# Reordering the first routing of a macaron block and moving VectorE work to GpSimd and ScalarE

## The reference

```
x = x + 0.5 * L0_ffn(layernorm(x))    # 8 experts, 2 per row, d_ff 512
x = x + L0_attn(layernorm(x))         # 16 heads of 8, softmax over 256 keys
x = x + 0.5 * L0_ffn(layernorm(x))    # the same experts again
x = x + 0.5 * L1_ffn(layernorm(x))    # channel mix with the row before, r * (relu(k)^2 Wv)
x = x + L1_attn(layernorm(x))         # gated Toeplitz product by FFT along the sequence
x = x + 0.5 * L1_ffn(layernorm(x))
```

## Time and profile before

| | us |
|---|---|
| median of 3 runs | 720.45 (718.42 to 724.24) |
| the profiled execution | 716.23 |
| its span in the trace | 714.5 |
| PE, DVE, ACT, POOL busy | 603.1, 458.4, 336.7, 300.2 |

### The profile page before, as it was taken

The page is one execution under the profiler, slowest core; times in us unless marked ns, Lnnn a source line. Parts: engine busy times, 40 slices in busy tenths (PEclk is TensorE's granted clock), DMA queues, the critical chain, the costliest instruction groups (busy, mean ns, idle before and its releaser), DMA issues.

```text
span 714.5 us, 12146 instructions
## 1 busy us (share of the span) xinstructions
PE 603.1 (84%) x4067; PEld 472.4 (66%) x4067; DVE 458.4 (64%) x1226; ACT 336.7 (47%) x808; POOL 300.2 (42%) x396
## 2 busy tenths in 40 slices
PE   3516998897999898899988977999899899987795
PEld 3514787776897554555445644699688788966694
DVE  3896753342586765878887663368335587688675
ACT  2641443442464567546653243644243457445434
POOL 2634646566582502120010252254567574763251
PEclk9555899998999999879997585999899999998698
DMA  8611102111400000201000020014111300020000
GB/s 304 194 58 52 38 20 41 34 38 37 119 26 20 30 1 9 63 1 31 1 30 1 4 63 18 21 20 140 38 34 46 93 24 20 24 75 22 9 1 30
DMA packets 30459, 32.70 MB, mean 46 GB/s; under 512 B 5408, under 2 KB 24256, under 8 KB 30400
## 3 DMA queue, kind: packets, MB, share of 16 engines
q1 hardware_dynamic: 23648, 19.68, 8.5%
q0 software_dynamic: 5888, 12.07, 6.7%
q10 hardware_dynamic: 864, 0.18, 0.1%
HBM read 20.64 MB, written 11.27 MB: 45 GB/s over the span
## 4 chain that ended last, share of the span: by engine, by line
PE 63%; DVE 15%; another core or an unknown queue 5%; POOL 5%; issue 5%; ACT 4%; DMA 3%; SPq 1%; ACTq 0%; DVEq 0%
PE bank L1800 10%; PE bank L1709 9%; PE bank L1716 5%; PE bank L1859 5%; PE bank L1815 4%; PE bank L1850 3%; PE bank L1831 3%; PE bank L1782 3%; PE bank L1789 3%; PE bank L1763 3%; PE bank L1784 3%; PE bank L1787 2%; PE bank L1783 2%; PE bank L1788 2%
## 5 line engine op out<-in xcount | busy, mean ns | idle before, releaser
L1150 POOL DMA_INDIRECT XROW<-rows_in,of x92 | 91.6, 996 | 75.0 <-PE bank L1709 30.6
L1157 POOL DMA_INDIRECT rows_out<-OROW,to x92 | 93.1, 1012 | 68.6 <-DVE OROW L1559 46.6
L1547 DVE TENSOR_TENSOR SGA<-bank,SGA 128x512 f32<-128x512 f32 x92 | 62.4, 687 | 76.4 <-PE bank L1789 49.9
L1800 PE MATMUL bank<-WD,AT 128*128 x736 | 96.9, 279 | 0.9 <-DVE AT L1551 0.9
L1591 DVE TENSOR_REDUCE BIG<-bank 128x4 f32<-128x1024 f32 x64 | 77.4, 1222 | 29.7 <-PE bank L1831 29.5
L1800 PEld LDWEIGHTS bank<-WD,AT 128*128 128x128 f32 x736 | 92.2, 195 | 3.9 <-issue 1.3
L1246 ACT ACTIVATE SGA<-bank 128x512 f32<-128x512 f32 x92 | 54.7, 600 | 65.6 <-PE bank L1784 47.2
L1289 ACT ACTIVATE BIG<-bank 128x1024 f32<-128x1024 f32 x64 | 64.9, 1022 | 42.4 <-PE bank L1850 39.1
L1250 ACT ACTIVATE AT<-bank 128x512 f32<-128x512 f32 x58 | 34.5, 597 | 60.6 <-PE bank L1709 33.1
L1110 POOL TENSOR_SCALAR stats<-stats 128x4 f32<-128x4 f32 (+1 forms) x15 | 3.6, 238 | 135.4 <-DVE stats L1381 128.5
L1709 PE MATMUL bank<-ident,SGA 128*128 128x128 f32 x368 | 54.3, 277 | 3.2 <-DVE AT L1551 2.2
(11 more groups left out here) (224 smaller groups left out, 1359.3 us busy)
## 6 DMA issues: line engine op xcount, KB each, us to landing
rows_in<-HROW SPq DMA_DIRECT2D x16, 256.0 KB
GO<-rows_out SPq DMA_DIRECT2D x16, 256.0 KB
BIG<-in_w_e_dram SPq DMA_DIRECT2D x7, 512.0 KB, 10.1
WD<-in_w_e_dram SPq DMA_DIRECT2D x1, 2048.0 KB, 17.8
XROW<-rows_in,of POOLq DMA_INDIRECT x92
rows_out<-OROW,to POOLq DMA_INDIRECT x92
X<-in_x_dram SPq DMA_DIRECT2D x4, 256.0 KB, 8.6
out_dram<-X SPq DMA_DIRECT2D x8, 128.0 KB, 1.9
```

The costliest lines, as they stand in the source:

```text
L1150: gp.indirect_dma_start(cut(v.xrow[st.to.i], u % 4), None, v.hs[k], bass.IndirectOffsetOnAxis(ap=v.of[k % 2][:, u:u + 1], axis=0)).then_in ...
L1157: gp.indirect_dma_start(v.outs[k], bass.IndirectOffsetOnAxis(ap=v.to[k % 2][:, u:u + 1], axis=0), cut(v.orow[st.xt.i], u % 4), None).then_ ...
L1547: ve.tensor_tensor(a, bk[:, :], a, ALU.mult).then_inc(s["gated"], 1)
L1800: x = pe.matmul(cut(bk, u % 4), cut(v.aT[st.xt.i], f), cut(mine, f), start=(f == 0), stop=(f == 3))
```

## The change

- **Order.** `RANKS` becomes a list by group. Routing of group 0 and the constants have rank -29; the first quad has 3 - 30 = -27. `k_diag` to `k_enorm`, `decayed` and the `prep` of tiles 2 and 3 no longer start by the clock but when the first quad's `x_lo` is planned (mark "begun"). `prep(0)` and `prep(1)` start at 4.3 and 9.6. A pair of tiles counts as picked after `g_pick`, no longer after `g_mix`; the small gating tensors are doubled for this.
- **Choice of engine.** A wish may name a second operation (`other`). Whichever engine the plan finds free first takes it, ACT before DVE before POOL: `n_apply` or `n_pool` (POOL), `s_apply` or `s_pool` (POOL), `h_rows` or `h_act` (ACT).
- **p_lo moves.** ACT writes a second scaled copy of the projected bank (`p_raw`, 128x512), and POOL adds it to the rounded one. The ring of q and k pairs has three instead of four; the memory goes to two `raw` tiles.
- **Splits.** DVE and POOL make 8 remainders each (11 and 5 before). Rank 0 instead of 3.
- **r_place** handles both picks in one product and one sum: 13 operations instead of 15.
- **Tables.** `QUOTA` of exp 2 instead of 6, `PATIENCE` 0.3 instead of 1.0.

```diff
-QUOTA = {"silu": 2, "exp": 6}
-PATIENCE = 1.0
-RANKS = {"route": -6.0, "route1": 0.0, "combine": -3.0, "quads": 3.0, "settle": 2.0, "attention": -6.0, "experts": 0.0, "layer": 0.0}
+QUOTA = {"silu": 2, "exp": 2}
+PATIENCE = 0.3
+RANKS = {"split": 0.0, "decayed": 0.0, "route": [-29.0, 0.0, -6.0, -6.0], "quads": [3.0, 4.0, 9.0, 3.0],
+         "experts": [0.0, 0.0, 0.0, 1.0], "settle": [10.0, 9.0, 3.0, 0.0],
+         "combine": [-3.0, -3.0, -3.0, 12.0], "attention": [-6.0, -6.0], "layer": [0.0, -4.0]}
...
-        st = yield from self.add("n_apply", {"to": self.xns}, q=c, own=own, src=st)
+        st = yield from self.add("n_apply", {"to": self.xns}, "n_pool", q=c, own=own, src=st)
...
-        yield 40.0
+        self.begin(self.scales())
+
+    def scales(self):
+        yield from self.until("begun")
...
-            st = yield from self.add("w_lo2" if (2 * e + j) % 3 == 2 else "w_lo", e=e, j=j, src=st)
+            st = yield from self.add("w_lo2" if j else "w_lo", e=e, j=j, src=st)
...
+        elif k < 2:
+            yield 4.3 + 5.3 * k
         else:
-            yield 4.0 + 1.5 * k + 3.0 * (k > 1)
+            yield from self.until("begun")
...
-        st = yield from self.add("h_rows", bank=bk, to=h, own=own, src=st)
+        st = yield from self.add("h_rows", {}, "h_act", bank=bk, to=h, own=own, src=st)
...
+        if n == 0:
+            self.mark("begun", st)
...
+                raw = yield from self.add("p_raw", {"xt": self.raws}, j=j, bank=mm.bank, src=mm)
                 st = yield from self.add("p_hi", take, j=j, bank=mm.bank, src=mm, **to)
...
-                st = yield from self.add("p_lo", j=j, bank=mm.bank, src=st, **to)
-                self.banks.give(mm.bank, st)
+                st = yield from self.add("p_lo", j=j, xt=raw.xt, src=st, **to)
+                self.raws.give(raw.xt, st)
...
     def decayed(self):
 
-        yield 20.0
+        yield from self.until("begun")
...
-        st = yield from self.add("s_apply", {"to": self.xnq}, n=n, q=q, src=st)
+        st = yield from self.add("s_apply", {"to": self.xnq}, "s_pool", n=n, q=q, src=st)
...
+            for t in range(4):
+                x = gp.tensor_scalar(cut(v.xn[st.to.i], t), v.X[:, 4 * q + t, :], v.st2[i][:, t, 0:1],
+                                     v.rs[i][:, t:t + 1], ALU.subtract, ALU.mult)
...
+            gp.tensor_tensor(x[:, :], v.raw[st.xt.i][:, :], x[:, :].bitcast(F32), ALU.add).then_inc(s["p_lo"], 1)
...
+            for t in range(4):
+                x = act.activation(cut(v.hrow[st.to.i], t), cut(bk, t), ACT.Copy, scale=v.zr[st.own.i][:, t:t + 1])
...
-            for i in range(2):
-                chain(ve.tensor_tensor(v.r64, v.picks[k % 2][i], te, ALU.mult))
-                chain(ve.tensor_reduce(v.rplace[:, 8 * i:8 * i + 8], v.r64, AX.X, ALU.add))
+            chain(ve.tensor_tensor(v.r128, v.picked[k % 2], te.unsqueeze(1).broadcast_to([128, 2, 8, E]), ALU.mult))
+            chain(ve.tensor_reduce(v.rplace.rearrange("p (i t) -> p i t", i=2), v.r128, AX.X, ALU.add))
```

More of the change, by code:

```diff
@@ L56 @@
  d_turn .23 d_mm .45 c_mm .9 s_turn .23 m_mm 1.0 m_vmm .45 y_uv .9 y_dft 1.8 y_idft 1.8 y_turn .23 y_mm .45""",
-    "ACT": """k_evac .3 k_comb .3 k_enorm .6 n_evac .6 z_ss 1.9 w_hi .63 x_hi .7 silu .6 a_act .6 o_ss 1.9 g_tanh .25
- p_ss 1.9 p_T .7 p_hi .78 v_rows .6 st_exp 1.03 os_out .6 cc_evac .6 d_sig .3 d_ln .3 d_exp .6 d_act .3
+    "ACT": """k_evac .3 k_comb .3 k_enorm .6 n_evac .6 z_ss 1.9 h_act 1.2 w_hi .63 x_hi .7 silu .6 a_act .6 o_ss 1.9 g_tanh .25
+ p_ss 1.9 p_T .7 p_raw .7 p_hi .78 v_rows .6 st_exp 1.03 os_out .6 cc_evac .6 d_sig .3 d_ln .3 d_exp .6 d_act .3
  d_evac .4 d_silu .3 c_evac .4 s_evac .4 m_left .9 m_gate 1.2 y_silu .6 y_fw .6 y_evac .4""",
     "DVE": """k_scale .1 k_counts .4 k_diag 1.4 n_stats 1.4 n_apply 1.15 g_copy .3 h_rows 1.15 g_rank 2.1 g_pick 1.2 g_mix .3
- r_scan .3 r_place 5.2 r_hot .6 r_ids .8 r_tables 1.4 x_lo .75 w_lo .7 gated .7 a_dve .7 o_rows 1.6 mix 2.7 p_x 1.15 p_lo .75 mx_max 1.23 nm_add .41
+ r_scan .3 r_place 4.6 r_hot .6 r_ids .8 r_tables 1.4 x_lo .75 w_lo .7 gated .7 a_dve .7 o_rows 1.6 mix 2.7 p_x 1.15 mx_max 1.23 nm_add .41
  cc_part .6 at_x .7 d_gamma .2 d_in .2 d_stats .6 d_rows 1.2 d_tt .4 omega .1 s_stats 1 s_apply .7 m_mix .95 m_out .85
  y_prods 1.4 y_prod .95 y_gate .4 y_x .4""",
-    "POOL": """n_rstd 1.3 z_rstd 1.3 w_lo2 1.6 fetch 1.27 o_rstd 1.3 spread 1.27 p_rstd 1.3 d_rstd 1 s_rstd 1
+    "POOL": """n_rstd 1.3 n_pool 1.8 s_pool .95 p_lo 1.45 z_rstd 1.3 w_lo2 1.6 fetch 1.27 o_rstd 1.3 spread 1.27 p_rstd 1.3 d_rstd 1 s_rstd 1
  m_zero .1 y_cross 1.8""",
@@ L164 @@
     at: float = 0.0
+    other: str = None
 class Plan:
@@ L224, in go_on @@
             return
+        rank = self.rank
         if isinstance(until, float):
@@ L229, in go_on @@
             self.wishes[LENGTH[until.do][0]].append(until)
+            if until.other:
+                self.wishes[LENGTH[until.other][0]].append(until)
         else:
@@ L240, in serve @@
         one = min(ready, key=lambda w: (w.at + w.rank, w.number))
-        self.wishes[engine].remove(one)
+        self.wishes[LENGTH[one.do][0]].remove(one)
+        if one.other:
+            self.wishes[LENGTH[one.other][0]].remove(one)
+            if LENGTH[one.other][0] == engine:
+                one.do = one.other
         slots = {}
@@ L271, in slot, with add @@
         return min(free, key=lambda s: s.done)
-    def add(self, do, take={}, **what):
+    def add(self, do, take={}, other=None, **what):
+        self.number += 1
+        wish = Wish(do, 0, self.number, None, take, other=other)
+        slots = yield wish
+        do = wish.do
         engine, length = LENGTH[do]
-        self.number += 1
-        slots = yield Wish(do, 0, self.number, None, take)
         at = self.count[do] = self.count.get(do, 0) + 1
@@ L463, in quads @@
             g, i = divmod(n, QUADS)
+            if n:
+                self.rank = RANKS["quads"][g]
             ids = yield from self.until(("routed", g))
@@ L634, in projects @@
         for c in range(4):
+            self.rank = RANKS["attention"][c // 2]
             yield from self.project(c)
@@ L640, in attention @@
         for u in range(32):
+            self.rank = RANKS["attention"][u // 16]
             ev = yield from self.until(("projected", u // 2))
@@ L889, in layer @@
         for q in range(8):
-            self.begin(self.sequence(q))
+            self.begin(self.sequence(q), RANKS["layer"][q // 4])
 def the_plan():
     p = Plan()
-    p.begin(p.constants(), 0.0)
-    p.begin(p.decayed(), 0.0)
+    p.begin(p.constants(), RANKS["route"][0])
+    p.begin(p.decayed(), RANKS["decayed"])
     for e in range(E):
-        p.begin(p.split(e), 3.0)
+        p.begin(p.split(e), RANKS["split"])
     for g in range(4):
-        p.begin(p.route(g), RANKS["route1" if g == 1 else "route"])
-        p.begin(p.experts(g), RANKS["experts"])
-        p.begin(p.combine(g), RANKS["combine"])
-    p.begin(p.quads(), RANKS["quads"])
-    p.begin(p.attention(), RANKS["attention"])
-    p.begin(p.layer(), RANKS["layer"])
+        p.begin(p.route(g), RANKS["route"][g])
+        p.begin(p.experts(g), RANKS["experts"][g])
+        p.begin(p.combine(g), RANKS["combine"][g])
+    p.begin(p.quads(), RANKS["quads"][0] - 30.0)
+    p.begin(p.attention())
+    p.begin(p.layer(), RANKS["layer"][0])
     p.run()
@@ L1135, in gpsimd_program @@
             root(v.rs[i], v.var[i], v.st2[i][:, :, 1], 1.0, EPS_LN, 4).then_inc(s["n_rstd"], 1)
+        elif st.do == "n_pool":
+            i = st.own.i
+            w.wait_ge(s["n_rstd"], st.src.at)
+            w.wait_ge(s[st.to.by], st.to.at)
+            for t in range(4):
+                x = gp.tensor_scalar(cut(v.xn[st.to.i], t), v.X[:, 4 * q + t, :], v.st2[i][:, t, 0:1],
+                                     v.rs[i][:, t:t + 1], ALU.subtract, ALU.mult)
+            x.then_inc(s["n_pool"], 1)
+        elif st.do == "s_pool":
+            w.wait_ge(s["s_rstd"], st.src.at)
+            w.wait_ge(s[st.to.by], st.to.at)
+            for t in range(2):
+                x = gp.tensor_scalar(cut(v.xnq[st.to.i], t), v.X[:, 2 * q + t, :], v.q2[n][:, t, 0:1],
+                                     v.qrs[n][:, t:t + 1], ALU.subtract, ALU.mult)
+            x.then_inc(s["s_pool"], 1)
+        elif st.do == "p_lo":
+            w.wait_ge(s["p_hi"], st.src.at)
+            x = v.trips[st.to.i][st.j]
+            gp.tensor_tensor(x[:, :], v.raw[st.xt.i][:, :], x[:, :].bitcast(F32), ALU.add).then_inc(s["p_lo"], 1)
         elif st.do == "z_rstd":
```

96 lines of the change are left out of this document (53 added, 43 removed).

## The result

The changed kernel takes 726.13 us in the median of five runs (721.49 to 727.24), the kernel before 719.38 on the same chip (710.49 to 724.24, five runs). I had forecast 701. The profiled execution took 721.49, its span 719.7.

A forecast was written before the change was run, and what follows sets the result against it. Start bound by waits for VectorE, experts by TensorE, attention by neither fully; -19.8 + 8 + 3 - 6 - 4 = -18.8 from 716.2 gives 697.4, plus 4.2 for a median 701.6, given as 701; range 690 to 711.

The forecast's parts named there:

- Part 3, p_lo: Attention: low parts leave VectorE for GpSimd, ScalarE's extra passes hidden, longer pair latency covered; -4 us.
- Part 1, the start: Up to the first expert product: earlier root, gating, scan and routing bring it from 74.9 to 55.1, 19.8 us gained.
- What is paid back: Experts' stretch: held back work returns where TensorE is full, +8 us, and table loads between silus, +3.
- Part 2, quota: Start of attention: with exp quota 2, group 1's last block gets in some 19 us earlier, worth -6 us.
- Part 4: The end: `s_pool` and the last group's ranks move order only; 0, between -3 and +12 us.
- The slower one: Attention's projections: POOL, busy with group 2's fetches, delays chunk 3's `p_lo`; +32 us, 738; chance 0.10.
- The port: Attention's routings: GpSimd work on the port shared with VectorE stretches some 13 VectorE operations; +13 us, 714; chance 0.10.
- The last combine's late results: The end: the last combine's rank of 12 lets up to 12 us of other work go ahead; 713; chance 0.10.
- More: Attention: VectorE's relief and earlier tiles keep TensorE's clock up, gaining 15 us more; 686 or less; chance 0.14.

The follow-up runs named there:

- x3: Kernel before with only the low parts' move (`p_raw` on ScalarE, `p_lo` on GpSimd, three pairs), quiet chip: 695.10 us, ratio 1.034.
- x1: Kernel before, unchanged, on the quiet chip: 668.03 us, ratio 0.995.
- x2: Changed kernel, unchanged, on the quiet chip: 688.52 us, ratio 1.026.
- x4: Changed kernel with the low parts back on VectorE and four pairs, quiet chip: 673.20 us, ratio 1.000.
- The third round: Changed kernel without `s_pool`, 725.75 us; that with settling ranks of before, 735.21; kernel before with `s_pool`, 719.05; changed kernel unchanged, 723.99.
- e4: Kernel before with the new start alone, old quota and patience, low parts and norms on VectorE, quiet chip: 702.95 us, ratio 1.048.
- s1: Changed kernel without `s_pool`, so the layer's norms are all on VectorE: 725.75 us, ratio 1.009.
- e2: Changed kernel with the last group's and the layer's ranks of before, quiet chip: 689.36 us, ratio 1.033.
- s2: Kernel before with `s_pool` offered for `s_apply` and nothing else: 719.05 us, ratio 1.015.
- e1: Changed kernel without `n_pool` and `s_pool`, every norm on VectorE, quiet chip: 709.55 us, ratio 1.063.

## Why the prediction was wrong, step by step

- **Part 3, p_lo: the step that failed.** I took -4 from a range of -20.8 to 0, with the longer latency "covered, unless POOL is late". Measured +23 alone and +15 within the change (quiet chip): my range had no positive end, since I took the longer way of a pair and ScalarE's 32 passes as covered and hidden. I had read the maxima's 25.9 us of waits for TensorE as "the relief is worth little", and not drawn the other conclusion: in a stretch in which no engine is full, each waits for the others, and an edit that adds work and way between them can lose. In x3, 10 us of the loss are TensorE's idle time and 16 its lower clock (183.05 and 171.26 busy at 0.89 and 0.79 lose 20 and 36 us). How the edit makes TensorE idle stays open. The longer way alone is not shown to do it: from a pair's first projection to its second low part it is 1.7 us more in the mean (11.1 for 9.4, x3 and x1) and 1.3 (10.3 for 9.0, x2 and x4), not the 2.8 that I had estimated, because a low part on VectorE had begun only 0.8 to 1.0 us after its rounded tile (median of 32) and on GpSimd begins 0.1 us after it; and TensorE waited 0.8 us for low parts in x3. The waits that grew are for ScalarE's exponentials and VectorE's maxima, and in which of the three ways (ScalarE's passes, the pair's way, the new order) the edit lengthens them no run separates.
- **Part 1, the start.** First product -15.2 for -19.8. Root and gating came earlier than forecast (17.5, 18.9), but two tiles' gating took 13.5 us, not 8.4: four weight remainders of 0.6 stand between its steps, and three operations are stretched from 0.42 to 1.4 or 1.5, each beside a remainder of GpSimd (from 20.55 and from 26.49). `r_place` took 6.0 for 4.4, the inversions 8.3 for 8.1, and from there to the product 11.0 for 12.5. The trace thus agrees at the start with what the Trainium skill ("SBUF — State Buffer", "SBUF: two separate sides") says of the port pair that VectorE and GpSimd share, and more of it was on the path than the single row I had counted.
- **What is paid back.** 11 forecast, leaving 9; at block 23 8.6 us of the 15.2 were paid back and 6.6 left (7.6 and 7.2 on the quiet chip), so this term was too large rather than too small. On the quiet chip (x1, x2) TensorE is busy 33.05 and 19.80 us up to the first product, and from it to block 23:

```profile
74.65:142.96 68.31, 68.28 (x442) 60.79 (x442) 35.70 (x84) 31.94 (x80) 42.91 (x49) 0.96 0.16 38
59.82:135.80 75.98, 74.87 (x490) 65.90 (x490) 51.66 (x170) 42.97 (x115) 48.60 (x58) 1.00 0.19 45
```

  Some 13.3 us of work at the low clock were moved and 6.6 came back at the full one, half, as I had told; TensorE's idle time up to block 23 hardly changed (41.6 and 41.1). What the sum had wrong is that the 9 us would reach the end. Tile 0's first result already comes 2 to 3 us later than before (206.5 for 203.7; 189.5 for 187.3), and in x4, without the low parts' move, the layer is reached 1 us later than in x1. The third round shows that the settling rank holds tile 0 back, and also that taking it away gains nothing. The table loads fell between silus just as told, six of them, 7.7 us of ScalarE.
- **Part 2, quota.** Mechanism right (14 and 11 us earlier), value 1 us alone instead of 6: even the later result (323.4 without the edit) was there before attention's second chunk ended at 347.9, so nothing waited for it. Whether it matters when the start is moved is not shown: e4, which kept the old quota, got the block only at 296.
- **Part 4.** 0 forecast; the layer stretch takes 144 us in the changed kernel for 136 to 140 in the kernel before, 143.4 without `s_pool` (s1), 145.8 with the tail ranks of before (e2), the kernel before with `s_pool` takes 145.3 (s2), x3, which has neither, 143.6, and x4 even 148.4. So 4 to 6 us of the loss lie here, within my bounds of -3 and +12. Several things lengthen it, and which one does in the changed kernel stays open.
- **The rivals.** The slower one named the right part and the wrong mechanism: each low part began within 1.3 us of its rounded tile, and the maxima waited some 1 us for it in all. The port held little in attention: the maxima stayed at 1.22, also the 21 of 64 that ran beside a low part in x3, and all other VectorE operations together were stretched by some 4 to 6 us (the worst, the four one-hots of a routing, from 0.68 to 1.17 in the changed kernel's first trace), not 13. The last combine's late results (658.7 for 647.3, with the earlier trace rows's mix in its place) are real and cost nothing that e2 could find. "More" (clock up by relief) was the reverse of what came.

## What to carry to other kernels

In a stretch where no engine is full, count what an edit adds (passes, hops, way between engines) before the busy time that it takes off one, and give the range a losing end; the engine whose waits are ended by another is not the one to relieve. Read a gain at a milestone where the same work is done in both kernels: block 24 looked level although the changed kernel had 24 more `down` products behind it. Compare parts one at a time on one chip, beside both whole kernels: the change as a whole doesn't show that one part of it costs 15 us.

## What the runs showed of the hardware

- The same kernel takes 668 us on some chips and 717 on others. On the second kind 3 to 6% of the chain is time in which an instruction of ScalarE or VectorE is late for no recorded reason, mostly in the expert stretches; here in the kernel before on the first chip:

```profile
164.00 0.69 ACT XHI L1238
164.68 3.34 another core or an unknown queue
168.06 4.26 another core or an unknown queue
172.35 0.60 ACT AT L1250
```

  In the stretch from 75 to 235 us TensorE is busy 147.2 of 160 there and 159.1 on the quiet chip. What they are was not settled. From the quiet chip to the first the changed kernel's span grows by 33 us (686.4 to 719.7) and that of the kernel before by 53 (661.5 to 714.5), so that by medians the change looks like +0.9% on one and +2.4% on the other. The entry itself holds 34 and 37 us of these spans: it doesn't explain the whole difference.
- GpSimd takes 0.81 to 0.88 us for a 128x128 subtract and multiply with two scalars per row (0.34 on VectorE) and 1.27 us for a 128x512 sum, the planner having counted 1.8 for a norm of four that takes 3.2. Still the kernel with these norms was 20 us faster than the one without (e2 and e1).
- The granted clock in the profile can read 1.00 over a start in which the products last as at 0.50 (the changed kernel up to its first gate product, there and in x2): the length of a known product is the better witness.
